# A transformer block with 16 experts: expert rows scattered to token order while they are made

## What is computed

```python
x = x + cross_attention(layernorm(x), ctx)      # 16 heads of 16
x = x + self_attention(layernorm(x))            # 16 heads of 16, causal
h = layernorm(x)
shared = silu(h @ shared_gate) * (h @ shared_up) @ shared_down
p, i = top_k(softmax(h @ router_w), 2)          # 2 of 16 experts
routed = sum over k of p[k] * (silu(h @ gate[i[k]]) * (h @ up[i[k]])) @ down[i[k]]
out = x + shared + routed
```

## Time and profile before

| | |
|---|---|
| median of 3 runs | 1461.71 us (1458.19 to 1462.27) |
| profiled execution | 1460.17 us, span 1458.4 us |
| busy, share of the span | PE 85%, DVE 68%, ACT 47%, POOL 30% |
| mean granted TensorE clock | 0.926 |
| moved by DMA | 91.73 MB, mean 63 GB/s |
| loop until the first slot | 0 to about 1233 us |
| 80 slots | about 1233 to 1368 us |
| combine | 1368 to 1458 us |

### The profile page before, as it was taken

How to read it: one execution, slowest core, us unless ns; L and a number is a source line. 1 busy time by engine, 2 the same in 40 slices (tenths; PEclk the granted TensorE clock), 3 DMA queues, 4 the chain that set the end, 5 groups by cost and what they waited for, 6 DMA issues and landing times.

```text
span 1458.4 us, 55455 instructions
## 1 busy us (share of the span) xinstructions
PE 1246.7 (85%) x22808; PEld 1027.7 (70%) x22808; DVE 986.1 (68%) x2480; ACT 680.5 (47%) x1265; POOL 435.4 (30%) x420
## 2 busy tenths in 40 slices
PE   2378999999999999999999999999999865999400
PEld 2367888788878888888888878888888643888300
DVE  4146777777777777777777777777777544655433
ACT  0225555555555555555555555555555421444200
POOL 1112233333333333333333333333333121000376
PEclk7559999999999999999999999999999985999755
DMA  6610011111001111110111111111110004455476
GB/s 212 178 32 20 28 32 32 31 32 31 32 31 32 32 35 33 47 32 32 35 32 35 32 32 32 31 32 32 32 36 18 13 19 157 154 160 167 147 201 185
DMA packets 74963, 91.73 MB, mean 63 GB/s; under 512 B 9072, under 2 KB 66416, under 8 KB 74480
## 3 DMA queue, kind: packets, MB, share of 16 engines
q1 hardware_dynamic: 68592, 71.57, 16.0%
q0 software_dynamic: 6144, 16.79, 3.9%
HBM read 58.70 MB, written 33.82 MB: 63 GB/s over the span
## 4 chain that ended last, share of the span: by engine, by line
PE 79%; DVE 8%; POOL 4%; issue 4%; DMA 2%; SPq 2%; ACT 1%; POOLq 0%; DVEq 0%; ACTq 0%
PE ringB L479 16%; PE ringC L490 13%; PE oA L572 10%; PE banksS L555 9%; DVE mx L1172 5%; PE banksS L764 5%; PE banksS L519 4%; POOL pt L1043 3%; PE ringB L653 3%; PE ringB L607 2%; PE banksS L624 2%; PE ringB L639 2%; PE oA L479 2%; PE ringB L474 2%; PE banksS L534 2%
## 5 line engine op out<-in xcount | busy, mean ns | idle before, releaser
L490 PE MATMUL ringC<-wx_kv,ct 128*128 128x256 f32 x512 | 160.9, 314 | 39.2 <-DVE kc L1122 24.5
L844 ACT ACTIVATE pt<-banksS 128x1024 f32<-128x1024 f32 x128 | 127.7, 1023 | 129.7 <-PE banksS L555 118.4
L1006 POOL TENSOR_TENSOR kn<-kc,rr 128x512 f32<-128x512 f32 x64 | 66.7, 1063 | 333.7 <-DVE rr L1160 333.7
L1172 DVE TENSOR_REDUCE mx<-banksS 128x8 f32<-128x2048 f32 x64 | 146.4, 2287 | 3.1 <-PE banksS L534 3.1
L490 PE MATMUL ringC<-wx_kv_rest,ct 128*128 128x256 f32 x512 | 147.9, 289 | 0.0
L490 PE MATMUL ringC<-wx_kv,ct_rest 128*128 128x256 f32 x512 | 147.6, 288 | 0.0
L490 PEld LDWEIGHTS ringC<-wx_kv,ct 128*128 128x128 f32 x512 | 100.3, 196 | 53.4 <-DVE kc L1122 25.4
L555 PE MATMUL banksS<-qT,kT 17*128 17x64 f32 x4096 | 133.6, 279 | 0.9 <-DVE qT L1177 0.9
L555 PEld LDWEIGHTS banksS<-qT,kT 17*128 17x128 f32 x4096 | 124.7, 192 | 8.0 <-issue 1.4
L1000 POOL TENSOR_TENSOR sc<-sc,rz 128x1024 f32<-128x1024 f32 x32 | 62.4, 1950 | 223.7 <-DVE rz L1233 223.7
L1043 POOL DMA_INDIRECT pt<-expert_rows,pos_y x64 | 63.2, 988 | 165.6 <-DMA expert_rows<-kc 146.4
(11 more groups left out here) (208 smaller groups left out, 2927.9 us busy)
## 6 DMA issues: line engine op xcount, KB each, us to landing
ct_in<-in_ctxT SPq DMA_DIRECT2D x64, 256.0 KB, 3.4
pt<-rows_by_expert SPq DMA_DIRECT2D x80, 128.0 KB, 2.1
expert_rows<-kc SPq DMA_DIRECT2D x80, 128.0 KB, 2.0
xt<-in_x SPq DMA_DIRECT2D x32, 128.0 KB, 3.6
rows_without_experts<-base SPq DMA_DIRECT2D x32, 128.0 KB, 1.8
rows_by_expert<-zeros SPq DMA_DIRECT2D x16, 256.0 KB, 3.7
kT<-rows_without_experts SPq DMA_DIRECT2D x32, 128.0 KB, 3.1
out<-ksq SPq DMA_DIRECT2D x32, 128.0 KB, 2.6
```

What stands on the lines that cost most here:

```text
L490: mm = pe.matmul(ringC[:, half * DIM:(half + 1) * DIM], left[:, p, k, j // 2, (j % 2) * P:(j % 2 + 1) * P], right[:, k, part * DIM:(part + ...
L844: act.activation(pt[:, g, :, :, :, :].rearrange("p i q c n -> p i (q c n)"), banksS[:, :, g * 256:(g + 1) * 256], ACT.Exp)\
L1006: pool.tensor_tensor(kn[:, 2 * jj:2 * jj + 2, :, 0:HD].rearrange("p j h d -> p (j h) d"), kc[:, 2 * jj:2 * jj + 2, :].rearrange("p j (h d) ...
L1172: dve.tensor_reduce(mx[:, 2 * r:2 * r + 2, :, HD].rearrange("p q i -> p i q"), banksS[:, :, :].rearrange("p i (q m) -> p i q m", q=2), AX. ...
```

## The change

- The expert rows go straight to token order. `expert_rows` gets two neighbouring rows for each token, number 2*token + k, and room for padding rows behind them. In the slots GpSimd scatters each slot's 128 rows of y there, in place of SP's 80 stores.
- A row must know its destination: the rows of h get four more numbers (1040 bytes in place of 1024), the first being 2*token + k. There are two copies of h for k = 0 and 1: SP loads the numbers of a tile from a constant input (`row_numbers`, behind `store_base`, pieces of 16 bytes), ACT copies the row to the second (`row_copied`), the scatters wait for them. In the slots ACT copies the number column into `row_to`.
- Padding rows come from inputs (`pad_rows`, `dump_rows`) with numbers that lead into the room behind the tokens' rows; the nine stores of zeros are one copy from DRAM to DRAM behind the loads of the weights. The pads of each expert are copied as before, with 1040 bytes a row.
- The slot table is made in five chunks of 16 slots: the first ahead of the slots, the others one operation per slot in the slots 0 to 23. `rows_found` and `pos_y` are gone; the two operations for `coef` stand in the slots 40 and 44.
- The scaling of w_down moves from behind the table into step 34 of the loop.
- The combine has no gathers: SP loads each tile's pair of rows (128 x 2 KB) and its base, 8 buffers each, the first 8 base tiles during the slots; ACT issues the stores of the result.

```diff
-FIRST_SLOTS = E
+CHUNK = 16
+RING = 8
+ROW = DIM + 4
+PADS = 2 * P
+DUMP = 2 * TOK
...
-        h = sb("h", [P, 2, DIM])
+        h = sb("h", [P, 2, 2, ROW])
...
+        row_to = sb("row_to", [P, SLOTS], U32)
...
-            def clear_rows():
-
-                sp.wait_ge(setup_dve, 1)
-                sp.dma_start(zeros_d.rearrange("(p q) d -> p q d", q=2), h[:, :, :]).then_inc(zeros_out, 16)
-                for n in range(E // 2):
-                    at = E * ROOM + 2 * n * P
-                    sp.dma_start(rows_d[at:at + 2 * P, :].rearrange("(p q) d -> p q d", q=2), h[:, :, :]).then_inc(zeros_out, 16)
+            def row_numbers(d, p):
+
+                freed(sp, ev[f"scattered{p}"], d, buffers=2)
+                here = number_t[d] if isinstance(d, int) else number_t[bass.ds(d, 1), :, :, :].rearrange("o p k n -> p (o k) n")
+                sp.dma_start(h[:, p, :, DIM:ROW], here).then_inc(number_in[p], 16)
...
-                    sp.dma_start(rows_d[bass.ds(at, 2 * P), :], zeros_d[:, :]).then_inc(pads_out, 16)
+                    at = sp.snap(row_at[e % DEEP], min_val=0, max_val=E * ROOM - PADS)
+                    sp.dma_start(rows_d[bass.ds(at, PADS), :], w["pad_rows"][e]).then_inc(pads_out, 16)
...
                 on(s, odd, 5, store_base)
+                on(s, odd, 5, row_numbers)
             row_at = [sp.alloc_register(f"row_at{c}") for c in range(DEEP)]
             load_cross_weights()
-            clear_rows()
+            sp.dma_start(rows_d[E * ROOM:E * ROOM + E * P, :], w["dump_rows"]).then_inc(dump_out, 16)
+            sp.wait_ge(setup_dve, 1)
             tiles(sp, step)
...
-                sp.wait_ge(slots_known, 1 if j < FIRST_SLOTS else 2)
+                sp.wait_ge(slots_known, j // CHUNK + 1)
                 if j >= DEEP:
-                    sp.wait_ge(ev["rows_turned"].sem, ev["rows_turned"].of(j - DEEP))
+                    sp.wait_ge(ev["rowsT_ready"].sem, ev["rowsT_ready"].of(j - DEEP))
...
-            for j in range(SLOTS + 2 * DEEP):
-                if j < SLOTS:
-                    load_slot(j)
-                if j >= 2 * DEEP:
-                    store_y(j - 2 * DEEP)
...
+            for j in range(SLOTS):
+                load_slot(j)
             sp.wait_ge(base_out, 16 * TILES)
...
+            for t in range(RING):
+                load_base(t)
+            for c in range(DEEP):
+                sp.wait_ge(y_out[c], 16 * SLOTS // DEEP)
+            for t in range(TILES):
+                c = t % RING
+                if t >= RING:
+                    sp.wait_ge(ev["res_ready"].sem, ev["res_ready"].of(t - RING))
+                    load_base(t)
+                sp.dma_start(yg[c // DEEP][:, c % DEEP, :, :], y_t[t]).then_inc(yg_in[c], 16)
...
+            def row_copied(d, p):
+                act.wait_ge(ev["h_ready"].sem, ev["h_ready"].of(d))
+                act.copy(h[:, p, 1, 0:DIM], h[:, p, 0, 0:DIM]).then_inc(ev["row_copied"].sem, 1)
...
+                    act.copy(column(row_to, i), xg[:, s, DIM:DIM + 1])
                     act.copy(xgT[:, s % 2, :], bank(s % 2)[:, 0:DIM]).then_inc(ev["rowsT_ready"].sem, 1)
...
+            for t in range(TILES):
+                c = t % DEEP
+                act.wait_ge(ev["res_ready"].sem, ev["res_ready"].of(t))
+                act.dma_start(out_t[t], res[:, c, :]).then_inc(out_done[c], 16)
...
                     pool.wait_ge(ev["pos_ready"].sem, ev["pos_ready"].of(d))
+                    pool.wait_ge(number_in[p], 16 * (d // 2 + 1))
+                else:
+                    pool.wait_ge(ev["row_copied"].sem, ev["row_copied"].of(d))
...
-            for t in range(TILES):
-                c = t % DEEP
-                if t >= DEEP:
-                    pool.wait_ge(yg_in[c], 32 * (t // DEEP))
-                    pool.wait_ge(ev["res_ready"].sem, ev["res_ready"].of(t - DEEP))
-                for k in range(2):
-                    pool.indirect_dma_start(out=yg[:, c, k, :], out_offset=None, in_=y_d[:, :],
-                                            in_offset=bass.IndirectOffsetOnAxis(ap=pos_y[:, 2 * t + k:2 * t + k + 1], axis=0))\
-                        .then_inc(yg_in[c], 16)
+            for j in range(SLOTS):
+                c = j % DEEP
+                pool.wait_ge(ev["y_ready"].sem, ev["y_ready"].of(j))
+                pool.indirect_dma_start(out=y_d[:, :], out_offset=bass.IndirectOffsetOnAxis(ap=row_to[:, j:j + 1], axis=0),
+                                        in_=y[:, c, :], in_offset=None).then_inc(y_out[c], 16)
...
             def step(s, odd):
-                if isinstance(s, int) and s == 2:
+                if s == TILES + 2:
+                    dve.wait_ge(expert_weights_in, 16 * 5)
+                    dve.tensor_scalar(w_down[:, :, :], w_down[:, :, :], 0.5, None, ALU.mult).then_inc(weights_set, 1)
...
             for j in range(SLOTS + 3):
                 expert(j, j % DEEP, j // DEEP)
-                if j in (8, 12, 16, 20, 24):
-                    rows_found((j - 8) // 4)
...
+                if j < 6 * (SLOTS // CHUNK - 1):
+                    slots_found(j % 6, 1 + j // 6)
```

More of the change, by code:

```diff
@@ L287, in perceiver_block @@
         ev.update(chain("prob_ready", "prob_ready"))
+        ev.update(chain("row_copied", "row_copied"))
         for p in range(2):
@@ L1364, in _, with slots_found @@
             link(dve.tensor_scalar(spare, filled, -1.0, float(ROOM), ALU.mult, ALU.add))
-            for lo, hi in ((0, FIRST_SLOTS), (FIRST_SLOTS, SLOTS)):
-                over, skipped = (past[0:1, k * 1024:k * 1024 + (hi - lo) * E].rearrange("p (j e) -> p j e", e=E) for k in range(2))
+            def slots_found(part, n):
+                lo, hi = n * CHUNK, (n + 1) * CHUNK
+                over, skipped = (past[0:1, k * CHUNK * E:(k + 1) * CHUNK * E].rearrange("p (j e) -> p j e", e=E) for k in range(2))
@@ L1373, in _ @@
-                link(dve.tensor_tensor(rows_at_i[0:1, lo:hi], rows_at[0:1, lo:hi], here, ALU.add))
-                link(dve.tensor_scalar(weights_at_i[0:1, lo:hi], weights_at[0:1, lo:hi], E - 1.0, float(DIM), ALU.min, ALU.mult))
-                dve.memset(top[:, :], 0.0).then_inc(slots_known, 1)
-            dve.wait_ge(expert_weights_in, 16 * 5)
-            dve.tensor_scalar(w_down[:, :, :], w_down[:, :, :], 0.5, None, ALU.mult).then_inc(weights_set, 1)
+                if part == 0:
+                    link(dve.tensor_tensor(over, end[0:1, :].unsqueeze(1).to_broadcast([1, CHUNK, E]),
+                                           here.unsqueeze(2).to_broadcast([1, CHUNK, E]), ALU.is_le))
+                elif part == 1:
+                    link(dve.tensor_tensor(skipped, over, spare[0:1, :].unsqueeze(1).to_broadcast([1, CHUNK, E]), ALU.mult))
+                elif part == 2:
+                    link(dve.tensor_reduce(rows_at[0:1, lo:hi], skipped, AX.X, ALU.add))
+                elif part == 3:
+                    link(dve.tensor_reduce(weights_at[0:1, lo:hi], over, AX.X, ALU.add))
+                elif part == 4:
+                    link(dve.tensor_tensor(rows_at_i[0:1, lo:hi], rows_at[0:1, lo:hi], here, ALU.add))
+                else:
+                    link(dve.tensor_scalar(weights_at_i[0:1, lo:hi], weights_at[0:1, lo:hi], E - 1.0, float(DIM), ALU.min, ALU.mult))
+                    dve.memset(top[:, :], 0.0).then_inc(slots_known, 1)
@@ L1379, in expert @@
+            for part in range(6):
+                slots_found(part, 0)
             def expert(j, c, n):
@@ new lines, in _ @@
+                if j == 40:
+                    link(dve.reciprocal(total[:, :], total[:, :]))
+                if j == 44:
+                    link(dve.tensor_tensor(coef[:, :, :], best[:, :, 0:2], total[:, :].unsqueeze(2).to_broadcast([P, TILES, 2]), ALU.mult))
+            for t in range(TILES):
+                c, q = t % DEEP, t % RING
+                dve.wait_ge(yg_in[q], 32 * (t // RING) + 32)
+                if t >= DEEP:
+                    dve.wait_ge(out_done[c], 16 * (t // DEEP))
+                both = yg[q // DEEP][:, q % DEEP, :, :]
+                dve.scalar_tensor_tensor(res[:, c, :], both[:, 0, :], coef[:, t, 0:1], base8[:, q, :], ALU.mult, ALU.add)\
@@ L1428, in combine @@
                     .then_inc(ev["half_summed"].sem, 1)
                 dve.wait_ge(ev["half_summed"].sem, ev["half_summed"].of(t))
-                dve.scalar_tensor_tensor(res[:, c, :], yg[:, c, 1, :], column(row(coef, t), 1), res[:, c, :], ALU.mult, ALU.add)\
+                dve.scalar_tensor_tensor(res[:, c, :], both[:, 1, :], coef[:, t, 1:2], res[:, c, :], ALU.mult, ALU.add)\
                     .then_inc(ev["res_ready"].sem, 1)
-            rounds(dve, TILES, combine)
 def laid_out(a):
@@ L1458, in laid_out, with numbered @@
     q = np.arange(N)
+    def numbered(lo, n):
+        m = np.zeros((n, ROW), f32)
+        m[:, DIM] = lo + np.arange(n)
+        return m
     d = {
```

101 lines of the change are left out of this document (31 added, 70 removed).

## The result

The changed kernel takes **1418.4 us** (median of 4 runs, 1417.05 to 1419.69) against 1460.9 for the kernel before: a ratio of 0.9711, 95% interval 0.9695 to 0.9728, so 42.6 us less. The profiled execution took 1417.05, its span is 1415.2. The forecast was 1421.

What follows compares the result with a forecast made beforehand. TensorE was taken to bound the attention and expert parts, GpSimd's gathers the last 90.7 us. Terms -35.3 - 1.8 - 1.0 - 2.4 = -40.5 took the profiled 1460.2 to 1419.7; forecast 1421 us, range 1410 to 1448.

Steps and rivals of the forecast that it cites:

- The combine: After the last copy of an expert row: without gathers, 55.4 us against 90.7, so -35.3 us.
- The head: Start of the combine: last scatters of expert rows land and SP wakes, 4.0 us before the loads.
- The seam: Between attention and expert parts: TensorE starts at 1231.0 instead of 1232.79, last scatter awaiting row numbers; -1.8 us.
- The expert part: The slots: five position-table steps gone, three slots back from 1.94 to 1.63 us; -1.0 us.
- The start: Kernel start: the first context load goes out at 11.3 instead of 16.38, so -2.4 us.
- The loop: The 32 loop steps: added number loads and row copies are covered by existing waits; 0 us.
- (a): Rival, combine: DMA engines not filled, 80 us at 195 GB/s, total 1452, or halfway 1436; chance 0.20.
- (b): Rival, loop: the row numbers land late and cost 13 us, total 1434; chance 0.06.
- (c): Rival, expert part: VectorE holds up GpSimd's scatters, slots take 2.25 us, +50, total 1471; chance 0.07.
- The lock that the Trainium skill states: While VectorE copies fp32 SBUF to SBUF in fast mode, GpSimd can't write its DMA descriptors.
- The scatter that I held against it: Earlier trace, loop: a scatter at 729.77 took 1.06 us beside a VectorE cast, showing no hold-up.
- (d): Rival, whole kernel: no change, (a) at its end and (b) together, 1465; chance 0.04.

Runs made afterwards that it cites:

- gathers64: The changed kernel with the combine's 32 plain loads of expert rows replaced by 64 GpSimd gathers of the same rows in token order; 1457.8 us.
- gathers32: The changed kernel with the combine's plain loads replaced by 32 GpSimd gathers, each of 128 pairs of rows, 2 KB a row number; 1425.5 us.
- numbers first: The changed kernel with SP's load of the row numbers issued ahead of its store of base; 1414.5 us.
- the kernel "both": The changed kernel with 32 base tiles loaded during the slots, eight result buffers, row numbers ahead of the store of base, pads one tile earlier; 1402.3 us.

## Why the prediction was right, point by point

**The combine, -35.3 predicted, -38.7 and -37.7 measured.** The mechanism, GpSimd as the bound and then the DMA engines, is shown by gathers64 and gathers32. The head was good: the last scatter landed 3.6 us after the last copy, 4.0 predicted. The term that was off is the rate. I put the 7.3 MB of base and results at 325 GB/s, the value of 1 KB pieces alone, took 8% off for mixing, and got 49 us; from 1375 to 1405 us the mixture of 2 KB and 1 KB pieces, reads and writes, ran at 392 GB/s, above either stretch of the earlier trace rows, at a share of 1.07. From the landing (1366.7) to the end it is 48.5 us, predicted 49 + 2.4 = 51.4. That these are so close is partly luck: all 15.7 MB at 392 GB/s would take 40 us, and the other 8.5 went into the slow pieces at both ends (256 GB/s at the start, 254 and 131 at the end), for which I had put 2.4. The result buffers, which I had not looked at, turned out as a second limit beside the first. The Trainium skill (Perfetto Trace Analysis, "Roofline") says that a single active core of trn2 can pull more than its 358 GB/s share of HBM and puts about 120% as the practical ceiling; by that rule the trace agrees, 392 being 109%.

**The seam, -1.8 predicted, -1.5 and -1.2 measured.** The step that named the next late thing was right, the scatter behind the row numbers. The numbers landed 2.5 us after the store's issue (0.40, then 2.1 from their own issue, which took SP 0.61 of it), as in the sum (0.35 + 0.4 + 1.8). What was longer is the step from the landing to the scatter, 0.76 us in place of 0.2. The kernel that issues the numbers first confirms the cause by taking 2.3 us off.

**The expert part, -1.0 predicted, -0.2 measured.** From the 5th gate product to the last it is 121.90 in place of 122.84 (second profiles 121.91 and 122.75), so the 0.9 us of `rows_found` are gone as predicted. But the first four take 7.59 in place of 6.86 (7.80 and 7.13), which I had not costed. Before, four slots were loaded when w_down released TensorE, and it turned the rows of two in one go; after, it starts with the first load and pauses 0.24 us for the second. The second product then still ran at a granted clock of 0.50 (the 1.2 GHz level), where before it had 1.00 (2.4 GHz), and took 1.70 us in place of 1.03 (second profiles 1.88 and 1.27). Windows around the start of the second product, before and after:

```profile
1236.30:1237.40 1.10, 1.10 (x8) 0.87 (x7) 0.57 (x2) 0.51 (x3) 0.00 (x0) 1.00 0.15 48
```

```profile
1231.90:1233.00 1.10, 1.10 (x5) 0.92 (x4) 0.78 (x3) 0.64 (x3) 0.00 (x0) 0.50 0.54 149
```

So the term of this part that was off is one I had not put in the sum: at which clock the first products run. The length of the pause does not explain it. In all 14 profiles TensorE starts the slots at the lower level. Where w_down released it, with four slots loaded (before twice, and the kernel with the table back on the path), the clock rose 3.5, 4.0 and 4.3 us after its first transpose and the first four gate products took 6.86, 7.13 and 7.23 us. Where a load released it, the clock rose after 3.8 to 6.6 us and they took 7.03 to 8.20. But among these the shortest, numbers first, had a pause too (0.14 us), and the kernels with pauses of 0.16 and 0.17 us took 8.20 and 7.94, longer than the changed kernel with 0.24 (7.59). Windows around the second product in numbers first (pause 0.14) and in the kernel "both" (0.16):

```profile
1229.50:1230.60 1.10, 1.10 (x8) 0.89 (x7) 0.90 (x3) 0.52 (x4) 0.00 (x0) 0.98 0.51 129
```

```profile
1235.30:1236.40 1.10, 1.10 (x5) 0.92 (x4) 0.84 (x3) 0.59 (x3) 0.00 (x0) 0.50 0.55 158
```

What sets the moment of the rise stays open; part of the 0.7 us may be chance. The later slots lost nothing to the new work of GpSimd, ACT and VectorE, as predicted. GpSimd's scatters there:

```profile
1298.63 0.95 POOL L1048 DMA_INDIRECT expert_rows<-kc,row_to  x1 [0.74 <-DVE kc L1415]
1300.19 0.95 POOL L1048 DMA_INDIRECT expert_rows<-kc,row_to  x1 [0.60 <-DVE kc L1415]
```

**The start, -2.4 predicted, -1.5 at the first cast, -2.2 at the third.** The cast still waits 0.65 us for its context; I had it land as soon as VectorE was free.

**The loop, 0 predicted, 0 measured.** The numbers land in 2.1 us, close to the end I took, and the scatter slips without anyone waiting for it.

**The rivals.** (a) A combine that doesn't fill the DMA engines: excluded, share 1.07. (b) Late numbers: they are late by 2 us a step, and numbers first shows that it costs nothing. (c) VectorE holding up GpSimd: the 80 scatters took 0.95 to 0.96 us each, and the slots from the fifth on kept 1.63 us but for one of 1.68. The one at 1300.19 ran beside VectorE's operations of 0.29 us at 1300.60 and 1300.92. The lock that the Trainium skill states (SBUF — State Buffer, "SBUF: two separate sides") did not show in either kernel; whether these operations of VectorE run in a mode that would take it, no run here tells. The scatter that I held against it is a weaker test than I wrote: it had started 0.24 us ahead of the cast, and the section gives the lock to whichever starts first. But in the changed kernel no scatter of the loop ran beside a cast, and they took the same 1.06 us. (d) fell with (a) and (b).

The sum of the terms was -40.5; measured behind the last `pos_u` are -40.3 (first profiles) and -39.1 (second), and 1.5 to 2.2 at the start. The predicted parts there were -38.1. That the forecast is so close rests in part on errors that cancel, which is luck: 2.4 to 3.4 us too little gain in the combine, 0.3 to 0.6 too much at the seam, 0.8 too much in the slots and up to 0.9 at the start.

## What to carry to other kernels

An indirect DMA of 128 rows cost GpSimd the same 0.95 us with 1 KB and with 2 KB rows: put it where that engine is idle beside a busier one, or make its rows longer, and count instructions before bytes. When a wait is taken off a path, look at the first microseconds behind it as well: here they ran at the lower clock and took 0.7 us more than before. Where two limits lie close together, taking away either one shows little; try both before the stage is called done.

## What the runs showed of the hardware

- Mixed reads and writes of 1 and 2 KB pieces ran faster (392 GB/s over 30 us) than the stretches of a single kind in the trace before (378 and 312 GB/s over 4 us).
- A gather of 128 rows takes GpSimd 0.95 us in the median (0.94 to 1.20) with 2 KB rows and with 1 KB rows; a scatter in the loop 1.06, in the slots 0.95.
- A DMA of 256 pieces of 16 bytes landed 2.1 us after the start of its issue, which took SP 0.55 to 0.61 us.
- Two executions of the changed kernel differed by 4.6 us at the end of the loop and by less than 0.3 us in every part behind it; two of the kernel before by 1.7, and by 1.0 in the combine.
- When TensorE began the slots after 7 to 15 us of idling, its granted clock was 0.50 in all 14 profiles, and it rose 3.5 to 6.6 us after the first transpose; two profiles of one program differed there by 0.4 to 0.5 us.
